# Two attention layers and an MLP on one core: where ScalarE and VectorE turn a norm's blocks, and where the second query weights are fetched

## The chip, the cores and the metric

One NeuronCore of a Trainium2 chip runs the whole program. The time is the device time of one execution in microseconds (us), as a median of several runs. Its engines are TensorE (PE in the profile; PEld is its weight load), VectorE (DVE), ScalarE (ACT), GpSimd (POOL) and SyncE (SP), whose only work here is to issue DMAs.

## The reference, cut to what matters

A batch of 8 items with 256 tokens of width 512 goes through a small linear attention (called the first attention here), two cross-attentions with 16 heads of 128, and an MLP of width 2048, each of the last three behind a layer norm.

```python
def _cross_attention(q_in, kv_in, wq, bq, wk, bk, wv, bv, wo, bo, bias_k, bias_v):
    qh = (q_in @ wq + bq).reshape(b, q_len, H, K)
    kh = (kv_in @ wk + bk).reshape(b, t, H, K)
    vh = (kv_in @ wv + bv).reshape(b, t, H, K)
    kh = jnp.concatenate([kh, broadcast(bias_k)], axis=1)
    vh = jnp.concatenate([vh, broadcast(bias_v)], axis=1)
    logits = jnp.einsum('bqhk,bthk->bhqt', qh, kh) / sqrt(K)
    weights = jax.nn.softmax(logits, axis=-1)
    ctx = jnp.einsum('bhqt,bthk->bqhk', weights, vh).reshape(b, q_len, H * K)
    return ctx @ wo + bo

def _forward(x, xf_1, xf_2, ...):
    x = x + _cross_attention(layer_norm(x), xf_1, ...)
    x = x + _cross_attention(layer_norm(x), xf_2, ...)
    return x + gelu(layer_norm(x) @ w_fc1 + b_fc1) @ w_fc2 + b_fc2
```

## The kernel before

Every fp32 product is made of three matmuls of fp32r parts (L582, L583, L584 of the profile): each operand is held as a high part and the rest, and something has to make the two parts. For data it is ScalarE that writes the high part and VectorE that writes the rest; for weights GpSimd writes both (a cast, L464, and a subtraction, L467).

The program has three stretches. The **front** (0 to about 796 us) makes keys and values of all heads, for both layers, and stores them in DRAM: a unit K is one block of keys, a unit V one block of values, and V units of the last group share TensorE's time with the start of the first norm. The **steps** (about 796 to 2031 us) are the attention: 64 steps s, 32 to a layer, each of two heads (a "body") for 512 tokens (a "chunk", of four). The **last part** is the MLP.

A step has four slots j = 0 to 3, and slot j of step s has item J = 4s + j, which is one head for 256 tokens. What TensorE does in a slot is written out by hand in `slot_order`, in this order: the logits of the item after (`L`, J + 1, tile S), the transposes of this item's probabilities (`T`, J, tile T), half of a projection, the product with the values of the item before (`P`, J - 1, tile O), and the other half. In slots 0 and 2 the projection is that of the next step's queries (`q`, from hT and the weights wqs); in slots 1 and 3 it is two tiles of the output projection (`w`, from oT and wos). All of these but L, T and P write one of four banks of PSUM, named U, used in turn: the unit numbered u waits until VectorE has taken what unit u - 4 left (`take`, semaphore `free`, which VectorE raises in the order of the units).

For an item J the chain is: logits (PE), `least_of` (DVE, L1032), `exponentials` (ACT, L848, two of them, with their sums), `inverted` (DVE, L1036), `divided`, which scales the item (ACT, L856, two), transposes (PE, L676), `turned_hi` (ACT, L866) and `turned_lo` (DVE, L1040), product (PE), `weighted_hi` (ACT, L875) and `weighted_lo` (DVE, L1047).

`norm_at(s)` names the steps that carry a norm too: s = 0 and 1 (the last two chunks of the first norm), 30 to 33 (all four chunks of the second) and 62 and 63 (the first two of the third). In such a step GpSimd's normalised rows z are transposed in four blocks, `Z` with ch = 0 to 3 (PE, L619, a U bank each): two in slot 1, one in slot 2 and one in slot 3. `rows(ch)` takes such a block: on ScalarE two operations (L815 scale and offset into aff, L818 the high part hT), on VectorE one (L1005, the rest of hT, both of whose inputs lie in SBUF). VectorE also gathers statistics for the next norm (`stats_of`, L944; `moments`, L950 and L952) in those steps whose following step has a norm, 29 to 32, 62 and 63.

GpSimd's queue (in program order, around step 0): `normalise(0, 2)`, then `queries(1)` (the parts of the second query weights, into wqs_b, which shares its place with the buffer tmp and so waits until all V units have been staged), then `normalise(0, 3)`, then `add_bias(0, 1)` to `(0, 3)`, twelve additions of a bias row to x (L536). `normalise(0, 3)` also waits for block 3 of the chunk before it to have been transposed, since z has one buffer. SyncE's queue is in order too; `load(0, use(E), wa[E])` fetches the query weights of body E into raw[0] and first waits for GpSimd to have split what lay there.

Of the kernel before, what the change touches and what calls it, by code (L numbers as in the profile page):

```python
# [50 lines left out]
GROUPS = HBODIES // 2  # L51
# [134 lines left out]
def bass_xattn(nc, x_in, ctx_in, thw, thb, pgw, pgb, www, bncol, wa, wk, wv, wb, hcol, vrow,  # L186
               lncol, f1col, orow, out):
    ctx = ExitStack()
    with ctx:
# [6 lines left out]
        def f(ap):  # L196

            return ap.bitcast(F32)
# [97 lines left out]
        def bank(*name):  # L296
            return U[:, UNIT[name] % RING, :]
# [32 lines left out]
        def use(E):  # L330

            return 2 * GROUPS + E
# [3 lines left out]
        def _(sp):  # L336
            def load(i, n, src):

                if n:
                    sp.wait_ge(split[i], n)  # L340
                sp.dma_start(raw[i][:], src).then_inc(raw_in[i], 16)

            def load_o(E):
                load(1, use(E), wb[E].rearrange("p c (a n) -> p (c a) n", n=256))

            def load_v(e):

                for i in range(2):
                    load(i, 2 * e + 1, wv[2 * e + i])
                if e:  # L350
                    sp.wait_ge(vb_ready, e)
                sp.dma_start(raw_vb[:].rearrange("p a b n -> p (a b) n"),
                             vrow[2 * e:2 * e + 2].rearrange("a b n -> (a b) n").partition_broadcast(P)).then_inc(vrow_in, 16)
# [36 lines left out]
            for what, *a in FRONT:  # L390
                if what == "K":
                    e, c, h = a
                    n = KV["K", e, c, h]
                    sp.wait_ge(free, UNIT["K", e, c, h] + 1)
                    sp.dma_start(kd[2 * e + h // 2, c, :, :, h % 2, :], f(stage[:, n % 4, :, :])).then_inc(sent[n % 4], 16)
                    if (c, h) == (2, 0):
                        if e + 1 < GROUPS:
                            for i in range(2):
                                load(i, 2 * e + 2, wk[2 * e + 2 + i])
                        else:  # L400
                            load(0, use(0), wa[0])
                            load_o(0)
                    if (c, h) == (3, 2) and 0 < e < GROUPS - 1:
                        load_x(e + 1)
                elif what == "V":
                    e, t = a
                    n = KV["V", e, t]
                    sp.wait_ge(staged, VS["V", e, t] + 1)
                    sp.dma_start(vd[e, t // 4, :, :, :, t % 4, :].rearrange("p g q n -> p (g q) n"),
                                 f(value_slots(n)).rearrange("p g q n -> p (g q) n")).then_inc(sent[n % 4], 16)  # L410
                    if t == 8 and e + 1 < GROUPS:
                        load_v(e + 1)
                    if t == 12 and e == 0:
                        load_x(1)
                    if t == 2 and e + 1 == GROUPS:

                        sp.wait_ge(z_x, TILES)
                        for i in range(4):
                            sp.wait_ge(sent[i], 16 * 8)
                        load_k(0)  # L420
                        load_values(0)
# [1 line left out]
                sp.wait_ge(sent[i], 16 * len(KV) // 4)  # L423
            load_k(1)
            load_values(1)
            load(0, use(1), wa[1])

            for E in range(HBODIES):
                for c in range(CHUNKS):
# [328 lines left out]
        def _(act):  # L758
# [47 lines left out]
            def rows(n, c, ch):  # L806
                k = (n * CHUNKS + c) * CH + ch
                act.wait_ge(unit, UNIT["Z", n, c, ch] + 1)
                if k > 1:
                    former = [u for u in UNIT if u[0] == "Z"][k - 2]  # L810
                    act.wait_ge(free, UNIT[former] + 1)
                else:
                    act.wait_ge(z_x, TILES)
                col = n * CH + ch
                act.activation(aff[:, k % 2, :], bank("Z", n, c, ch), ACT.Identity, bias=lnc[:, 1, col:col + 1],  # L815
                               scale=lnc[:, 0, col:col + 1]).then_inc(ln_affine, 1)
                act.wait_ge(ln_affine, k + 1)
                act.activation(hT[:, 0, ch, columns(c)], aff[:, k % 2, :], ACT.Copy).then_inc(ln_hi, 1)  # L818
# [76 lines left out]
            for s, j in SLOTS:  # L895
                J = 4 * s + j
                if j % 2 and s + 1 < STEPS:
                    queries(s + 1, j // 2)
                elif j % 2:
                    hidden(0, j // 2)  # L900
                turned_hi(J)
                if J + 1 < ITEMS:
                    exponentials(J + 1)
                z_of = norm_at(s)
                if z_of and j > 1:
                    rows(*z_of, j - 1)
                if J:
                    weighted_hi(J - 1)
                if J + 1 < ITEMS:
                    divided(J + 1)  # L910
                if z_of and j in (1, 3):
                    rows(*z_of, 0 if j == 1 else 3)

            for what, *a in last_order():
                if what == "P":
# [8 lines left out]
        def _(dve):  # L924
# [77 lines left out]
            def rows(n, c, ch):  # L1002
                k = (n * CHUNKS + c) * CH + ch
                dve.wait_ge(ln_hi, k + 1)
                dve.tensor_tensor(hT[:, 1, ch, columns(c)], aff[:, k % 2, :], f(hT[:, 0, ch, columns(c)]), ALU.subtract).then_inc(free, 1)  # L1005
# [63 lines left out]
            for s, j in SLOTS:  # L1069
                J = 4 * s + j  # L1070
                z_of, z_former, measured = norm_at(s), norm_at(s - 1), norm_at(s + 1) if s else None
                if j == 0 and s:
                    if z_former:
                        rows(*z_former, 3)
                    output("w", s - 1, 1)
                elif j == 2 and s:
                    output("w", s - 1, 3)
                if J + 1 < ITEMS:
                    least_of(J + 1)
                if j % 2 and s + 1 < STEPS:  # L1080
                    queries(s + 1, j // 2)
                elif j % 2:
                    hidden(0, j // 2)
                turned_lo(J)
                if j == 1 and s:
                    output("w", s - 1, 2)
                elif j == 3 and not z_of:
                    output("w", s, 0)
                if J + 1 < ITEMS:
                    inverted(J + 1)  # L1090
                if z_of and j > 1:
                    rows(*z_of, j - 1)
                if J:
                    weighted_lo(J - 1)
                if z_of and j == 1:
                    rows(*z_of, 0)
                if z_of and j == 3:
                    output("w", s, 0)
                if measured and s > 1:
                    for t in ((0, 1), (2,), (3,), ())[j]:  # L1100
                        stats_of(s - 1, t)
                    if j == 2:
                        moments(*measured)
# [77 lines left out]
```

## Time and profile before

| | us |
|---|---|
| median of 3 runs | 2394.86 |
| the three runs | 2382.49, 2394.86, 2408.23 |
| the profiled execution's own time | 2395.99 |
| its span, first to last instruction | 2394.1 |
| PE busy in the span | 2351.6 (98%) |
| DVE busy | 1339.3 (56%) |
| ACT busy | 1143.8 (48%) |
| POOL busy | 462.4 (19%) |
| mean granted clock of TensorE | 0.996 |

The profile is of one execution; 1.9 us of its time lie outside its span. Busy TensorE is not TensorE at its peak: an end is modelled, and at the lower of its two clocks (0.50 in the profile, 1.2 GHz) the same matmuls are busy for longer.

### The profile page before, as it was taken

What the parts mean: (1) busy time and instruction counts of PE and PEld (TensorE: products, weight loads), DVE (VectorE), ACT (ScalarE), POOL (GpSimd) and SP (SyncE); (2) the same over time, 40 slices, a digit from 0 to 9 for tenths busy, and PEclk for the clock granted to TensorE, in tenths of its full rate; (3) what the DMA queues carried; (4) which work ended last, traced back from release to release, by engine and by line L of the source; (5) the groups of instructions that cost most, each with busy time, mean ns of one, the idle gap of its engine ahead of it and who ended that gap; (6) DMA issues with size and microseconds to landing.
All of it is one profiled execution on the core that took longest, in us unless ns stands there. A gap on an engine that the chain in (4) does not pass through costs nothing.

```text
span 2394.1 us, 32423 instructions
## 1 busy us (share of the span) xinstructions
PE 2351.6 (98%) x12304; PEld 1997.9 (83%) x12304; DVE 1339.3 (56%) x2328; ACT 1143.8 (48%) x2717; POOL 462.4 (19%) x280
## 2 busy tenths in 40 slices
PE   8999999999999899999999989999999999999999
PEld 7888888888888788888888878888888887788887
DVE  4544445445445666666666676666666666644433
ACT  3222222222223566666666677666666667422222
POOL 2121112112123501111001244111001115611110
PEclk9999999999999999999999999999999999999999
DMA  7555656566556424333333333333333331100001
GB/s 272 197 196 203 230 195 215 202 217 227 191 203 212 168 98 143 127 115 136 125 137 124 124 107 119 133 116 134 126 139 124 123 134 45 44 18 27 27 1 70
DMA packets 142168, 331.83 MB, mean 139 GB/s; under 512 B 8896, under 2 KB 74944, under 8 KB 125632
## 3 DMA queue, kind: packets, MB, share of 16 engines
q1 hardware_dynamic: 141296, 329.68, 39.3%
q8 instruction: 99, 1.62, 0.3%
q14 instruction: 53, 0.43, 0.1%
q10 hardware_dynamic: 720, 0.10, 0.0%
HBM read 190.81 MB, written 138.94 MB: 138 GB/s over the span
## 4 chain that ended last, share of the span: by engine, by line
PE 90%; DVE 4%; ACT 4%; DMA 1%; issue 1%; POOL 1%; ACTq 0%; SPq 0%; DVEq 0%; POOLq 0%
PE U L582 23%; PE U L584 23%; PE U L583 23%; PE T L676 4%; PE O L582 2%; PE O L584 2%; PE O L583 2%; PE S L584 2%; PE S L583 2%; PE S L582 2%; DVE hT L1005 1%; ACT aff L815 1%; DVE gT L1015 1%; ACT probs L856 1%; ACT hT L818 1%
## 5 line engine op out<-in xcount | busy, mean ns | idle before, releaser
L1024 DVE TENSOR_TENSOR x<-x,U 128x512 f32<-128x512 f32 x384 | 260.9, 683 | 79.9 <-PE U L584 77.5
L848 ACT ACTIVATE probs<-S,nm 128x257 f32<-128x257 f32 x512 | 237.7, 476 | 37.4 <-DVE nm L1032 37.4
L1032 DVE TENSOR_REDUCE nm<-S 128x2 f32<-128x514 f32 x256 | 177.3, 692 | 123.6 <-PE S L584 119.8
L866 ACT ACTIVATE PT<-T 128x512 fp32r<-128x512 f32 x256 | 152.5, 596 | 173.9 <-PE T L676 173.4
L856 ACT ACTIVATE probs<-probs,rs 128x256 f32<-128x256 f32 x512 | 230.1, 500 | 1.4 <-DVE rs L1036 1.1
L797 ACT ACTIVATE stage<-U,hc 128x512 fp32r<-128x512 f32 x128 | 88.1, 689 | 286.9 <-PE U L584 286.9
L989 DVE SCALAR_TENSOR_TENSOR stage<-U,hc,stage 128x512 fp32r<-128x512 f32 x128 | 96.2, 751 | 223.4 <-ACT stage L797 223.4
L582 PE MATMUL U<-cT,wks 128*128 128x512 f32 x512 | 214.0, 418 | 2.0 <-DVE cT L967 2.0
L582 PE MATMUL U<-wos,oT 128*128 128x512 f32 x512 | 214.2, 418 | 0.4 <-DVE oT L1047 0.4
L804 ACT ACTIVATE stage<-tmp 128x512 fp32r<-128x512 f32 x128 | 81.0, 633 | 271.1 <-DVE tmp L997 271.1
L1047 DVE SCALAR_TENSOR_TENSOR oT<-O,hc,oT 128x256 fp32r<-128x256 f32 x256 | 123.8, 484 | 147.5 <-ACT oT L875 147.3
L464 POOL CAST wos<-raw 128x1024 fp32r<-128x1024 f32 x20 | 20.8, 1039 | 954.1 <-PE U L584 954.1
L584 PE MATMUL U<-wos,oT 128*128 128x512 f32 x512 | 203.0, 397 | 0.0
L583 PE MATMUL U<-wos,oT 128*128 128x512 f32 x512 | 202.1, 395 | 0.0
L582 PE MATMUL U<-wvs,cT 128*128 128x512 f32 x512 | 201.7, 394 | 0.0
L584 PE MATMUL U<-cT,wks 128*128 128x512 f32 x512 | 200.4, 391 | 0.0
L583 PE MATMUL U<-cT,wks 128*128 128x512 f32 x512 | 200.2, 391 | 0.0
L584 PE MATMUL U<-wvs,cT 128*128 128x512 f32 x512 | 199.4, 390 | 0.0
L583 PE MATMUL U<-wvs,cT 128*128 128x512 f32 x512 | 199.4, 389 | 0.0
L1040 DVE TENSOR_TENSOR PT<-T,PT 128x512 fp32r<-128x512 f32 x256 | 175.5, 685 | 42.3 <-ACT PT L866 42.3
L875 ACT ACTIVATE oT<-O,hc 128x256 fp32r<-128x256 f32 x256 | 121.2, 473 | 130.8 <-PE O L584 130.6
L676 PE MATMUL T<-ident,probs 128*128 128x128 f32 x1024 | 155.3, 274 | 13.5 <-ACT probs L856 13.4
(166 smaller groups left out, 5827.1 us busy)
## 6 DMA issues: line engine op xcount, KB each, us to landing
kd<-stage SPq DMA_DIRECT2D x128, 516.0 KB, 3.1
kb<-kd SPq DMA_DIRECT2D x64, 1032.0 KB, 4.8
vd<-stage SPq DMA_DIRECT2D x128, 512.0 KB, 3.2
vb<-vd SPq DMA_DIRECT2D x64, 1024.0 KB, 5.0
raw<-wa SPq DMA_DIRECT2D x24, 512.0 KB, 5.9
raw<-wb SPq DMA_DIRECT2D x24, 512.0 KB, 5.9
raw<-wk SPq DMA_DIRECT2D x16, 512.0 KB, 5.9
raw<-wv SPq DMA_DIRECT2D x16, 512.0 KB, 5.7
```

Source lines behind the costliest of these rows:

```text
L582: pe.matmul(o, lhs[0], rhs[0], start=start, stop=False)
L583: pe.matmul(o, lhs[0], rhs[1], start=False, stop=False)
L584: return pe.matmul(o, lhs[1], rhs[0], start=False, stop=stop)
L676: mm = pe.transpose(T[:, at_:at_ + P], probs[:, J % 2, qt, tt * P:tt * P + P], ident[:])
L848: ins = act.activation(probs[:, r, qt, 0:257], S[:, qt, 0:257], ACT.Exp, bias=nm[:, r, qt:qt + 1], scale=-1.0, accum_out=sums[:, r, qt:qt ...
L856: ins = act.activation(probs[:, r, qt, 0:256], probs[:, r, qt, 0:256], ACT.Copy, scale=rs[:, r, qt:qt + 1])
L866: act.activation(PT[:, J % 2, 0, :], T[:], ACT.Copy).then_inc(pt_hi, 1)
L875: act.activation(oT[:, 0, h, b * 256:b * 256 + 256], O[:, 0:256], ACT.Identity, bias=hc[:, 3, at_:at_ + 1]).then_inc(o_hi, 1)
L1024: dve.tensor_tensor(x[:, tile, :], x[:, tile, :], bank(what, s, t), ALU.add).then_inc(free, 1)
L1032: dve.tensor_reduce(nm[:, J % 2, :], S[:, :, 0:257], AX.X, ALU.min).then_inc(least, 1)
L1040: dve.tensor_tensor(PT[:, J % 2, 1, :], T[:], f(PT[:, J % 2, 0, :]), ALU.subtract).then_inc(pt, 1)
L1047: dve.scalar_tensor_tensor(out=oT[:, 1, h, to], in0=O[:, 0:256], scalar=hc[:, 3, at_:at_ + 1], in1=f(oT[:, 0, h, to]), op0=ALU.add, op1=AL ...
```

## The change

ScalarE: in a step with a norm, `rows` comes behind `weighted_hi` and `divided` in every slot: block 0 in slot 1 (as before), block 1 in slot 2, blocks 2 and 3 in slot 3. VectorE: `rows` comes behind `weighted_lo` in slots 2 and 3 too, with the same blocks as before. SyncE: the second query weights are fetched behind the store of V unit 5 of the last group, not behind all stores and the first four loads of keys and values.

```diff
@@ -410,6 +410,8 @@
                     if t == 8 and e + 1 < GROUPS:
                         load_v(e + 1)
+                    if t == 5 and e + 1 == GROUPS:
+                        load(0, use(1), wa[1])
                     if t == 12 and e == 0:
                         load_x(1)
@@ -423,7 +425,6 @@
             load_k(1)
             load_values(1)
-            load(0, use(1), wa[1])
@@ -902,14 +903,13 @@
                 z_of = norm_at(s)
-                if z_of and j > 1:
-                    rows(*z_of, j - 1)
                 if J:
                     weighted_hi(J - 1)
                 if J + 1 < ITEMS:
                     divided(J + 1)
-                if z_of and j in (1, 3):
-                    rows(*z_of, 0 if j == 1 else 3)
+                if z_of:
+                    for ch in ((), (0,), (1,), (2, 3))[j]:
+                        rows(*z_of, ch)
@@ -1088,12 +1088,10 @@
                 if J + 1 < ITEMS:
                     inverted(J + 1)
-                if z_of and j > 1:
-                    rows(*z_of, j - 1)
                 if J:
                     weighted_lo(J - 1)
-                if z_of and j == 1:
-                    rows(*z_of, 0)
+                if z_of and j:
+                    rows(*z_of, j - 1)
                 if z_of and j == 3:
```

ScalarE's queue in step 31, from slot 2's `rows` to slot 3's, before (from L827 on it is slot 3; L856 is `divided`):

```order
L815 ACTIVATE aff<-U,lnc 128x512
L818 ACTIVATE hT<-aff 128x512
L875 ACTIVATE oT<-O,hc 128x256
L856 ACTIVATE probs<-probs,rs 128x256 x2
L827 ACTIVATE qT<-U,hc 128x512
L866 ACTIVATE PT<-T 128x512
L848 ACTIVATE probs,sums<-S,nm 128x257 x2
L815 ACTIVATE aff<-U,lnc 128x512
L818 ACTIVATE hT<-aff 128x512
L875 ACTIVATE oT<-O,hc 128x256
L856 ACTIVATE probs<-probs,rs 128x256 x2
L815 ACTIVATE aff<-U,lnc 128x512
```

The same place in the changed kernel, whose lines there have one number more:

```order
L876 ACTIVATE oT<-O,hc 128x256
L857 ACTIVATE probs<-probs,rs 128x256 x2
L816 ACTIVATE aff<-U,lnc 128x512
L819 ACTIVATE hT<-aff 128x512
L828 ACTIVATE qT<-U,hc 128x512
L867 ACTIVATE PT<-T 128x512
L849 ACTIVATE probs,sums<-S,nm 128x257 x2
L876 ACTIVATE oT<-O,hc 128x256
L857 ACTIVATE probs<-probs,rs 128x256 x2
L816 ACTIVATE aff<-U,lnc 128x512
L819 ACTIVATE hT<-aff 128x512
L816 ACTIVATE aff<-U,lnc 128x512
```

The pair for block 1 has moved behind `divided` in slot 2, and the pair for block 2 behind it in slot 3, where it now stands ahead of the pair for block 3.

VectorE's queue in slot 2 of step 31, and the start of slot 3 (from L1032 on), before:

```order
L1036 RECIPROCAL rs<-sums 128x2
L1005 TENSOR_TENSOR hT<-aff,hT 128x512
L1047 SCALAR_TENSOR_TENSOR oT<-O,hc,oT 128x256
L944 BN_STATS stats<-x 128x6
L950 BN_AGGR mv<-stats 128x2 x4
L952 TENSOR_SCALAR vpe<-mv 128x4
L1032 TENSOR_REDUCE nm<-S 128x2
L1010 SCALAR_TENSOR_TENSOR qT<-U,hc,qT 128x512
```

and in the changed kernel:

```order
L1036 RECIPROCAL rs<-sums 128x2
L1047 SCALAR_TENSOR_TENSOR oT<-O,hc,oT 128x256
L1005 TENSOR_TENSOR hT<-aff,hT 128x512
L944 BN_STATS stats<-x 128x6
L950 BN_AGGR mv<-stats 128x2 x4
L952 TENSOR_SCALAR vpe<-mv 128x4
L1032 TENSOR_REDUCE nm<-S 128x2
L1010 SCALAR_TENSOR_TENSOR qT<-U,hc,qT 128x512
```

L1005 has changed places with L1047; the statistics and the next `least_of` still stand behind it.

SyncE's queue from the last V stores to the first steps, before (stores vd<-stage, keys kb, values vb, query weights raw<-wa):

```order
L409 DMA vd<-stage 512x1x256 x13
L370 DMA kb_55<-kd 128x2064
L375 DMA vb_56<-vd 128x2048
L341 DMA raw<-wa 128x1024
L370 DMA kb_62<-kd 128x2064
```

and in the changed kernel:

```order
L409 DMA vd<-stage 512x1x256 x3
L341 DMA raw<-wa 128x1024
L409 DMA vd<-stage 512x1x256 x10
L370 DMA kb_55<-kd 128x2064
L375 DMA vb_56<-vd 128x2048
L370 DMA kb_62<-kd 128x2064
```

The fetch of the weights now stands ahead of the last ten stores. GpSimd's and TensorE's queues are the same in both kernels.

## Rows read from the trace of the kernel before

**Rows 1.** TensorE's waits: us in total, times, the longest.

```profile
PE T L676 <- ACT probs L856: 13.4, 16, 2.9
PE U L619 <- DVE hT L1005: 6.0, 1, 6.0
PE U L619 <- POOL z L528: 2.7, 1, 2.7
```

**Rows 2.** Stretches of 100 us: busy us and instructions of each engine, clock, DMA.

```profile
800.00:900.00 100.00, 87.90 (x506) 75.78 (x505) 66.32 (x103) 63.80 (x165) 30.66 (x21) 0.93 0.35 124
...
1000.00:1100.00 100.00, 100.00 (x607) 88.77 (x606) 63.25 (x119) 66.92 (x184) 6.82 (x4) 1.00 0.38 133
```

**Rows 3.** GpSimd in order of time around step 0: start, us, instruction, idle before.

```profile
810.45 1.04 POOL L464 CAST wqs_b<-raw 128x1024 fp32r<-128x1024 f32 x1 [14.06 <-DMA raw<-wa]
...
815.60 8.65 POOL L528 TENSOR_SCALAR z<-x,mv,rstd 128x512 f32<-128x512 f32 x4 [0.18 <-POOL rstd L519]
824.22 14.83 POOL L536 TENSOR_TENSOR x<-x,brow 128x512 f32<-128x512 f32 x12
```

**Rows 4.** SyncE's fetch of the weights, VectorE's last V unit, stores, TensorE's block 3.

```profile
801.21 0.42 SPq L341 DMA_DIRECT2D raw<-wa  x1
...
796.09 0.69 DVE L1000 TENSOR_TENSOR stage<-tmp,stage 128x512 fp32r<-128x512 f32 x1 [0.98 <-ACT stage L804]
...
vd<-stage SPq DMA_DIRECT2D x128, 512.0 KB, 3.2
...
811.17 0.60 PE L619 MATMUL U<-ident,z 128*128 128x128 f32 x4
```

**Rows 5.** Step 1: VectorE's and TensorE's rows in order of time, and a stretch.

```profile
829.13 10.46 DVE L1005 TENSOR_TENSOR hT<-aff,hT 128x512 fp32r<-128x512 f32 x1 [1.64 <-ACT hT L818]
...
839.65 1.11 PE L619 MATMUL U<-ident,z 128*128 128x128 f32 x4 [5.99 <-DVE hT L1005]
...
844.00:846.00 2.00, 1.60 (x6) 1.51 (x7) 1.65 (x3) 1.37 (x3) 0.00 (x0) 0.50 0.00 0
```

**Rows 6.** ScalarE in slots 2 and 3 of step 31, and slot 0 of step 32.

```profile
1406.25 0.48 ACT L848 ACTIVATE probs<-S,nm 128x257 f32<-128x257 f32 x1 [1.58 <-DVE nm L1032]
...
1407.17 0.78 ACT L815 ACTIVATE aff<-U,lnc 128x512 f32<-128x512 f32 x1
1407.97 0.63 ACT L818 ACTIVATE hT<-aff 128x512 fp32r<-128x512 f32 x1
1408.51 0.46 ACT L875 ACTIVATE oT<-O,hc 128x256 fp32r<-128x256 f32 x1
1408.87 0.90 ACT L856 ACTIVATE probs<-probs,rs 128x256 f32<-128x256 f32 x2
...
1411.43 0.48 ACT L848 ACTIVATE probs<-S,nm 128x257 f32<-128x257 f32 x1 [0.33 <-DVE nm L1032]
...
1418.24 0.48 ACT L848 ACTIVATE probs<-S,nm 128x257 f32<-128x257 f32 x1 [1.47 <-DVE nm L1032]
```

**Rows 7.** VectorE in slot 2 of step 31, up to slot 3's `least_of`.

```profile
1408.64 0.69 DVE L1005 TENSOR_TENSOR hT<-aff,hT 128x512 fp32r<-128x512 f32 x1 [1.17 <-ACT hT L818]
1409.25 0.48 DVE L1047 SCALAR_TENSOR_TENSOR oT<-O,hc,oT 128x256 fp32r<-128x256 f32 x1
1409.64 0.68 DVE L944 BATCH_NORM_STATS2 stats<-x 128x6 f32<-128x512 f32 x1
...
1410.72 0.68 DVE L1032 TENSOR_REDUCE nm<-S 128x2 f32<-128x514 f32 x1
```

**Rows 8.** TensorE: the transposes of slot 3, step 31, and the logits of slot 0, step 32.

```profile
1409.82 0.66 PE L676 MATMUL T<-ident,probs 128*128 128x128 f32 x4 [1.18 <-ACT probs L856]
...
1419.31 0.39 PE L582 MATMUL S<-kb,qT 128*128 128x258 f32 x1 [0.16 <-ACT probs L848]
```

**Rows 9.** The second norm's additions on GpSimd, and VectorE's L1005 beside them.

```profile
1445.75 15.86 POOL L536 TENSOR_TENSOR x<-x,brow 128x512 f32<-128x512 f32 x12
...
1451.10 1.50 DVE L1005 TENSOR_TENSOR hT<-aff,hT 128x512 fp32r<-128x512 f32 x1 [1.64 <-ACT hT L818]
```

## The prediction, made before the changed kernel ran

> **What bounds the kernel now.** I read the busy shares first, then TensorE's waits, then stretches of time, then single queues where they dip. TensorE is busy for 2351.6 of 2394.1 us, so all that any edit here can win is its idle 42.5 us and the time it ran at its lower clock. Most of the waits in its list belong to steps with a norm [rows 1]: 13.4 us for `divided` in 16 pieces, one of 6.0 for VectorE's part of a block, one of 2.7 for z. A stretch of steps without a norm has no idle time at all, while the one around the first norm lacks 12.1 us [rows 2]. Only the eight steps with a norm, and the approach to the first, are in question.
>
> **The moved fetch.** GpSimd is idle for 14.06 us because the second query weights are not there [rows 3]; they are asked for at 801.21 us, behind everything else [rows 4]. `normalise(0, 3)` stands behind them and starts at 815.60 [rows 3], and TensorE waits 2.7 us for its z. Fetched with V unit 5, some 759 us into the span, they have landed long before. GpSimd's split then waits for the last staged V (796.09 + 0.69 = 796.8) [rows 4] and is done by about 800.3, since the cast and subtraction take 3.5 us. What is late next is the one buffer z: block 3 of step 0 is transposed at 811.17 [rows 4], and 0.7 us behind that z may be written, so at 811.9; if step 0's wait of 0.95 us for `divided` goes too, at 810.8. Instead of 815.60, `normalise(0, 3)` starts 4.8 us earlier, ends at about 819.4, and TensorE, which wants the block at 821.5, does not wait.
>
> That 4.8 is also what reaches the end, though TensorE is first ahead by only 4.5. The twelve additions follow z directly; beside them VectorE's L1005 of block 0 took 10.46 us instead of 0.69, up to 0.5 us behind the last of them (824.22 + 14.83 = 839.05), and TensorE waited 5.99 for its bank and then ran at 0.50 of its clock [rows 3, 5]. The additions now start at 819.4 and end at 834.2, so VectorE is free at 834.75, not 839.59. TensorE arrives about 4.5 us earlier and waits as long as before. The stall itself is not removed, it moves. Term: **-4.8 us**, between -2.7 (the z wait alone, nothing else moving) and -6.5 (that wait, the 1.7 us lost to the lower clock behind it, and one us more of the next).
> The fetch itself adds 512 KB ahead of ten stores; GpSimd split raw[0] at 743.5, so SyncE does not wait there. A store lands 3.2 us after its issue [rows 4] (up to 9.6 beside the first keys and values), its slot is used again four units later, over 11 us. Zero, with at most 1 us if it lands in that crowd.
>
> **The moved operations, one step.** Take step 31 [rows 6 to 8]; starts that have no row are the next ones of the same queues. Before, ScalarE goes from the exponentials (1406.25) through two exponentials and their sums (0.92), L815 and L818 (1.34), L875 (0.36) and L856 to a start of the transposes at 1409.82, for which TensorE had been ready at 1408.5. Without the pair L815 and L818, `divided` ends at 1408.43: the transposes start at 1408.5. That wins 1.3 us, as meant, in slot 2 of every step with a norm.
>
> It is given back in the same step. VectorE's next `least_of` stands behind L1005, and L1005 behind ScalarE's L818. Exponentials to exponentials, before: 0.92 + 0.80 (L815) + 0.67 (until VectorE starts) + 0.61 (L1005) + 0.39 (L1047) + 1.08 (statistics) + 0.71 (`least_of`) = 5.18, as in the rows (1406.25 to 1411.43). After: 0.92 + 0.36 (L875) + 0.80 (L856) + 0.80 + 0.67 + 0.61 + 1.08 + 0.71 = 5.95, L1047 now lying in VectorE's idle time. So the next exponentials come 0.8 us later, at 1412.2.
> Slot 3 to slot 0: before 6.81 (1411.43 to 1418.24): both pairs and L875 and L856 lie between, and VectorE's L1005 of block 3, a residual addition and `least_of` behind them. After, the same operations in another order: 6.8 to 6.9. TensorE's logits there waited for these exponentials before (1419.31, wanted at 1419.0), so they come 0.84 us later. Its banks say the same: the second tile of w in slot 3 needs VectorE's q (L1010, now 1412.1 + 0.7 = 1412.8, wanted at 1411.6), and slot 0's q needs block 2's bank, freed at 1416.5 and wanted at 1415.5, because L815 and L818 of block 2 now lie behind `divided`. From there the rest of the step hangs on ScalarE and VectorE as before. Term per step with statistics in slot 2: **+0.8 us**; the bounds are -1.3 (nothing is given back) and +1.6.
>
> Steps 30, 31, 32 and 62 are such steps: +3.3. Step 0 has no statistics: exponentials to exponentials was 4.76 there, held by the transposes, and is 4.86; slot 0's q waits 1.0 for block 2's bank: 0. Step 1, behind the stall, by the same reckoning ends 0.8 later, since TensorE had no wait left to lose. Step 33 had two waits, 1.37 for `divided` and 0.41 for oT, which both go, and gets most back in the bank wait: -0.5. Step 63 has no item behind it, so there `divided` is 1.3 earlier (the longest wait of rows 1, 2.9 us), and what follows is held by the gelu in between: -1.1. **Sum: -4.8 + 0 + 0.8 + 3.3 - 0.5 - 1.1 = -2.3 us** against 2395.99, the profiled execution, which is 1.1 above the median: on the median's scale 2392.5.
>
> **A rule against the rows.** GpSimd's additions and VectorE's L1005, both with two inputs in SBUF, get in each other's way. In step 1 L1005 was held through nine additions of 1.27 us [rows 5]; in step 33, beside the same twelve additions, it took 1.50, so it got in behind the one that was running [rows 9].
> The Trainium skill, SBUF — State Buffer, Who interferes with whom, says that a VectorE instruction with two SBUF inputs and a GpSimd instruction that reads SBUF exclude each other, the second to start being blocked until the first has finished, which is one instruction. By that rule the trace agrees in step 33 and not in step 1, and the stall of step 1 would not be there after the change.
>
> **Rivals.**
> *The stall is luck, and does not come back.* L1005 at 825.3 gets in behind a running addition. TensorE then meets block 2's bank without a wait. In a step without the stall the transposes are 2.81 us ahead of the next exponentials (1403.44 to 1406.25 in step 31), in step 1 it was 11.21 (829.62 to 840.83), so 8.4 less, and some 1.2 of the lower clock: -9.6 more, 2383. For it: step 33, and the three runs, which lie 12.4 and 13.4 us apart, about one such stall each. Against it: in the front a row of the same kind (L1000 at 773.27, 4.25 us, beside `add_bias(0, 0)`) was held too, two of two in the first norm.
> *One more stall: slower.* The additions of the second norm (1445.75, 15.86 us) lie beside steps 32 and 33; VectorE's L1005 of block 1 now comes a us later against them, and if it, or block 0's, is held through the rest, TensorE loses 5 to 10 us. It decides whether L1005 is let in behind a running addition. 2392.5 + 9.6 = 2402. For it: the run at 2408.23. Against it: two of two got in there before.
> *The reorder does what it is for.* If VectorE is less tight than I reckon, 1.3 us remain won in each of eight steps: -4.8 - 10.4 = -15.2, 2380. Against it is the sum 5.18, which is exact.
> *No effect at all.* The fetch moves GpSimd, but something else holds z; the reorder cancels: 2395.
>
> **How the numbers follow.** My forecast, within 5 us of 2392.5, has 0.50; no stall 0.20; one more stall 0.17; the full gain 0.06; no effect 0.07. All but the ends lie between 2379 and 2404, which leaves out about 0.15. Two runs of this kernel differ by up to 1%, 24 us, so 1% is about what can be told from no change, and nothing above reaches it: under 2371 needs the full gain and two stalls less, over 2419 needs two more stalls. Faster 0.04, same 0.92, slower 0.04.
>
> **What would show it.** Right: GpSimd's cast into wqs_b near 797, z of `normalise(0, 3)` near 811, no wait of TensorE for z. In steps 30 to 32, transposes of slot 3 without a wait, but waits for banks (U, behind DVE) or for exponentials in slot 3 and slot 0, and steps of 23.4 us instead of 22.6. Wrong: a cast that still waits; steps of 21.3 us; a total that moves by more than the stalls can.

## The result, and the profile after

The changed kernel is slower: 2403.55 us (median of 22 runs, 2394.34 to 2405.09) against 2396.2 (22 runs, 2382.49 to 2408.23), a ratio of 1.0038 with a 95% interval of 1.0028 to 1.0048. The forecast was 2392.5. The change is within the 1% that counted as no change, and the range (to 2404) just holds the time, but the kernel moved the other way than forecast. The runs come in groups: of before, five at 2382.5 to 2387.9, sixteen at 2394.7 to 2397.6, one at 2408.23; of after, 21 at 2401.6 to 2405.1 and one at 2394.34. The profiled execution of after took 2403.1 us with a span of 2401.2.

TensorE's waits in the changed kernel (us in total, times, the longest), which answer to [rows 1]:

```profile
PE U L620 <- DVE hT L1005: 11.4, 2, 6.2
...
PE S L583 <- ACT probs L849: 5.4, 7, 1.7
PE U L583 <- DVE hT L1005: 4.9, 6, 0.9
PE T L677 <- ACT probs L857: 4.0, 11, 1.5
PE U L583 <- DVE qT L1010: 3.9, 4, 1.0
```

The wait for z is gone and that for `divided` has shrunk from 13.4 to 4.0 us. The waits for exponentials have grown from 4.1 to 5.4 us, six for block 2's bank and four for q have come, and, above all, there are two long waits for L1005 instead of one.

**First norm.** GpSimd in order of time, which answers to [rows 3], then SyncE's fetch and VectorE's L1005 of block 0 in step 1, which answer to [rows 4, 5]:

```profile
796.17 1.04 POOL L465 CAST wqs_b<-raw 128x1024 fp32r<-128x1024 f32 x1
797.30 2.39 POOL L468 TENSOR_TENSOR wqs_b<-raw,wqs_b 128x1024 fp32r<-128x1024 f32 x1
...
809.81 8.27 POOL L529 TENSOR_SCALAR z<-x,mv,rstd 128x512 f32<-128x512 f32 x4 [9.13 <-PE U L620]
...
759.48 0.66 SPq L341 DMA_DIRECT2D raw<-wa  x1
...
824.59 8.91 DVE L1005 TENSOR_TENSOR hT<-aff,hT 128x512 fp32r<-128x512 f32 x1 [1.64 <-ACT hT L819]
833.42 0.68 DVE L1024 TENSOR_TENSOR x<-x,U 128x512 f32<-128x512 f32 x1
```

The cast no longer waits; z starts 5.79 us earlier (815.60 against 809.81), which is 4.8 counted from the start of step 0 in each trace, and waits for TensorE's block 3. L1005 is held until the twelve additions are over, as forecast.

**A step.** ScalarE's exponentials in step 31, slots 2 and 3, and step 32, slot 0, which answer to [rows 6], with what lies between the first two:

```profile
1401.80 0.48 ACT L849 ACTIVATE probs<-S,nm 128x257 f32<-128x257 f32 x1 [1.57 <-DVE nm L1032]
...
1402.71 0.47 ACT L876 ACTIVATE oT<-O,hc 128x256 fp32r<-128x256 f32 x1
1403.07 0.91 ACT L857 ACTIVATE probs<-probs,rs 128x256 f32<-128x256 f32 x2
1403.87 0.78 ACT L816 ACTIVATE aff<-U,lnc 128x512 f32<-128x512 f32 x1
1404.68 0.63 ACT L819 ACTIVATE hT<-aff 128x512 fp32r<-128x512 f32 x1
...
1407.75 0.48 ACT L849 ACTIVATE probs<-S,nm 128x257 f32<-128x257 f32 x1 [1.38 <-DVE nm L1032]
...
1415.08 0.48 ACT L849 ACTIVATE probs<-S,nm 128x257 f32<-128x257 f32 x1 [1.94 <-DVE nm L1032]
```

Exponentials to exponentials are now 5.95 us, to the hundredth what was forecast, and 7.33 to slot 0, not 6.8 to 6.9. Against before, the three lie 4.45, 3.68 and 3.16 us ahead: the step loses 0.77 in slot 2 and 0.52 in slot 3. Of the second loss, 0.47 us is in VectorE's row of block 3, the second L1005 here:

```profile
1411.35 0.69 DVE L1005 TENSOR_TENSOR hT<-aff,hT 128x512 fp32r<-128x512 f32 x1 [1.69 <-ACT hT L819]
1411.96 0.68 DVE L1024 TENSOR_TENSOR x<-x,U 128x512 f32<-128x512 f32 x1
1412.68 1.16 DVE L1005 TENSOR_TENSOR hT<-aff,hT 128x512 fp32r<-128x512 f32 x1
1413.77 0.67 DVE L1024 TENSOR_TENSOR x<-x,U 128x512 f32<-128x512 f32 x1
1414.37 0.68 DVE L1032 TENSOR_REDUCE nm<-S 128x2 f32<-128x514 f32 x1
```

VectorE reaches slot 3's two L1005 late and close together, and the second, which began 0.14 us into one of GpSimd's z operations (2.08 us each, the second at 1412.54), took 1.16 us. Before, both lay beside z too, but began over 1.3 us into an operation, and took 0.69.

**Second norm.** GpSimd's additions and VectorE's L1005 of block 0 in step 33, which answer to [rows 9], TensorE's block behind it, and the stretch behind that (busy us and instructions of PE, PEld, DVE, ACT and POOL, then clock, DMA share, GB/s):

```profile
1442.73 14.88 POOL L537 TENSOR_TENSOR x<-x,brow 128x512 f32<-128x512 f32 x12
1457.57 1.03 POOL L465 CAST wqs_b<-raw 128x1024 fp32r<-128x1024 f32 x1
...
1449.25 9.89 DVE L1005 TENSOR_TENSOR hT<-aff,hT 128x512 fp32r<-128x512 f32 x1 [1.65 <-ACT hT L819]
1459.07 0.68 DVE L1024 TENSOR_TENSOR x<-x,U 128x512 f32<-128x512 f32 x1
...
1459.20 1.12 PE L620 MATMUL U<-ident,z 128*128 128x128 f32 x4 [6.19 <-DVE hT L1005]
...
1456.00:1464.00 8.00, 3.57 (x15) 3.20 (x16) 5.67 (x7) 3.59 (x10) 5.28 (x4) 0.50 0.00 0
```

This is where the sign turns. L1005 took 9.89 us and not 1.50: held through seven additions and the cast behind them. TensorE waited 6.19 us and then ran at half its clock, 1.2 GHz.

How far the changed kernel is ahead (-) or behind (+), from the starts of the same `least_of` in both traces: -0.97 at the start of step 0, -5.75 from the end of step 2 to step 30, -1.85 in slot 1 of step 33, +6.15 in step 34, still +6.16 ahead of step 62, +7.1 at the end.

### The profile page after: what moved, and what is told of

Its sections match the earlier page's. It is cut to its first block, busy times and chain, and to the rows that moved or that the text cites. A ratio compares the mean times of both kernels' runs of the same rounds, so it can differ in the third digit from the quotient of the medians.

```text
span 2401.2 us, 32423 instructions
## 1 busy us (share of the span) xinstructions
PE 2352.7 (98%) x12304; PEld 1996.0 (83%) x12304; DVE 1345.8 (56%) x2328; ACT 1144.3 (48%) x2717; POOL 459.2 (19%) x280
## 4 chain that ended last, share of the span: by engine, by line
PE 89%; DVE 4%; ACT 4%; issue 1%; POOL 0%; DMA 0%; ACTq 0%; DVEq 0%; POOLq 0%
PE U L583 23%; PE U L585 23%; PE U L584 23%; PE T L677 4%; PE S L583 2%; PE S L585 2%; PE S L584 2%; PE O L583 2%; PE O L585 2%; PE O L584 2%; DVE hT L1005 2%; ACT aff L816 1%; ACT probs L857 1%; ACT probs L849 1%; DVE gT L1015 1%
## 5 line engine op out<-in xcount | busy, mean ns | idle before, releaser
L1032 DVE TENSOR_REDUCE nm<-S 128x2 f32<-128x514 f32 x256 | 177.4, 693 | 123.4 <-PE S L585 119.6
L1047 DVE SCALAR_TENSOR_TENSOR oT<-O,hc,oT 128x256 fp32r<-128x256 f32 x256 | 123.9, 484 | 147.0 <-ACT oT L876 146.3
L583 PE MATMUL U<-hT,wqs 128*128 128x512 f32 x384 | 155.8, 406 | 6.7 <-DVE hT L1005 4.9
```

The lines of the kernel that those rows point to most:

```text
L583: pe.matmul(o, lhs[0], rhs[0], start=start, stop=False)
L1032: dve.tensor_reduce(nm[:, J % 2, :], S[:, :, 0:257], AX.X, ALU.min).then_inc(least, 1)
L1047: dve.scalar_tensor_tensor(out=oT[:, 1, h, to], in0=O[:, 0:256], scalar=hc[:, 3, at_:at_ + 1], in1=f(oT[:, 0, h, to]), op0=ALU.add, op1=AL ...
```

## The experiments

All ratios are to the kernel before, run on the same chip; they weigh all runs, and where the runs fall in groups they differ from the quotient of two medians. The kernels were not all run on one chip: the medians of before beside them lie between 2395.57 and 2396.46 us, so a difference of two medians below is uncertain by about 1 us from that alone. The part of the program ahead of step 0 also ends up to 4 us apart from one profile to another (794.3 to 798.1 us), so rows are compared step by step, from the first `least_of` of one step to that of the next. "Late additions" names an edit that several share, and that takes the additions of chunks 2 and 3 away from beside the held L1005:

```diff
                 for c in range(1, CHUNKS):
+                    if c == 2 and n < LAYERS:
+                        pool.wait_ge(free, UNIT["Z", n, CHUNKS - 1, CH - 1] + 1)
                     add_bias(n, c)
```

(and the same for n = 0, where the first norm's additions stand.) GpSimd does them once VectorE has taken the norm's last block.

### The two halves of the change

`fetch_only` is before with SyncE's lines of the change alone.

> Only the fetch of the second query weights is moved; ScalarE's and VectorE's order is that of before. Theory A (the changed kernel is slow because VectorE's L1005 of step 33 is now held through the second norm's additions, and the reorder brought it there): everything ahead of step 30 as in the changed kernel within 1 us, no long L1005 in step 33, 2396.2 - 5 = 2391. Rival B (the earlier start of the additions, which the fetch causes, is what lets L1005 be held wherever it meets them): a long L1005 in step 33 here too, about 2400. Rival C (neither: the reorder's waits alone are the loss): 2391 too, so the next run is needed to part A from C.

Measured: 2391.52 us (11 runs: eight at 2390.1 to 2393.6, three at 2402.8 to 2403.2), ratio 0.9996 (0.9973 to 1.0018). L1005 in step 1 and in step 33:

```profile
823.82 10.16 DVE L1006 TENSOR_TENSOR hT<-aff,hT 128x512 fp32r<-128x512 f32 x1 [1.64 <-ACT hT L819]
...
1445.90 1.44 DVE L1006 TENSOR_TENSOR hT<-aff,hT 128x512 fp32r<-128x512 f32 x1 [1.64 <-ACT hT L819]
```

The fetch alone is worth 4.5 us by the medians, but the interval reaches 5 us to either side, since the runs fall in two groups 11 to 12 us apart. The profiled one has the first L1005 held and the second let in, as before had; from the start of step 0 to that of step 3 it gains 3.7 us.

`reorder_only` is before with ScalarE's and VectorE's lines of the change alone.

> Only the order of ScalarE and VectorE is changed, the fetch stays where it was. Theory A: steps 30, 31, 32 and 62 are 1.3 us longer each (5.2 in all), and L1005 of step 33 is held for about 10 us, which costs 8: 2396.2 + 5 + 8 = 2409. If it is not held there, 2401. Rival B: 2401. Rival C: 2408 without any long L1005 behind step 1.

Measured: 2396.76 us (11 runs: nine at 2394.3 to 2397.6, 2407.98 and 2409.59), ratio 1.0019 (0.9997 to 1.0041). That is neither number as a median. The profiled execution is the one at 2409.59, and has both held:

```profile
828.98 11.27 DVE L1004 TENSOR_TENSOR hT<-aff,hT 128x512 fp32r<-128x512 f32 x1 [1.64 <-ACT hT L818]
...
1455.92 9.87 DVE L1004 TENSOR_TENSOR hT<-aff,hT 128x512 fp32r<-128x512 f32 x1 [1.64 <-ACT hT L818]
```

So both held costs 2409.6 here, and nine of eleven runs lie 12 to 15 us below that, about one held L1005 fewer. No profile of one was taken, so which of the two was let in there isn't shown. By their times both are held in two of eleven runs with the reorder alone, in three of eleven with the fetch alone, and in 21 of 22 with both halves. Which half brings the hold to step 33 is left open.

### Without the held L1005

`fetch_late` is `fetch_only` with late additions, `after_late` the changed kernel with them.

> Fetch moved, old order of ScalarE and VectorE, and in the first and second norm GpSimd's additions for chunks 2 and 3 wait until VectorE has taken the norm's last block, so that no L1005 of these norms can meet more than four additions. Theory A: no L1005 over 3 us in steps 0, 1 and 30 to 33; the stall of step 1 and its time at the lower clock go, about 9.6 us: 2391 - 10 = 2381, and all runs within 2 us of each other, since the runs of before at 2386 would be those without a stall. If the long L1005 only shows a wait that something else ends, it stays at 2391.

> The changed kernel with the same late additions. Theory A: both held L1005 go, leaving the reorder's own price of 1.3 us in each of steps 30, 31, 32 and 62, less 1 in step 63: 4 to 5 us above the run with the fetch moved and late additions, so 2385 to 2386, that is 17 below the changed kernel. Rival C (the reorder's waits are the whole loss): it stays near 2400, 10 or more above that run.

Measured: `fetch_late` 2378.63 us (7 runs, 2377.49 to 2381.23), ratio 0.9939 (0.992 to 0.9958); `after_late` 2382.97 (11 runs, 2381.0 to 2384.91), ratio 0.9964 (0.9947 to 0.9982). Every L1005 of `after_late` (duration in ns: least, median, most):

```profile
L1009 DVE TENSOR_TENSOR hT<-aff,hT x48: 691/693/2851, 754.8 to 2049.1; 128x512 fp32r<-128x512 f32 x48
```

None is held through a row of additions, and the runs no longer fall in groups: 4 us from the least to the most, where before has 26. With the holding gone, the reorder costs 2382.97 - 2378.63 = 4.3 us. From step 31's to step 32's first `least_of` it is 22.60 us without it and 23.90 with it. That +1.3 stands in steps 30, 31 and 62; step 32 shows only +0.3, since the late additions have made it 0.9 us longer in the old order (25.72 against 24.78 in before); steps 0, 1 and 33 add 0.7 together, and from step 63 on 1.7 us come back.

`after_late1` is the changed kernel with late additions in the second norm alone.

> The changed kernel with the additions late in the second norm alone. Theory A: only the held L1005 of step 33 goes, that of step 1 stays: 2403.5 less 8 to 10, so 2394 to 2395, and a few runs at 2384 in which step 1's is not held. If the two stalls hang together, 2384 or 2403.

Measured: 2393.47 us (10 runs, 2393.12 to 2394.07), ratio 0.9995 (0.9984 to 1.0007). None of the ten was near 2384, as a few were expected to be.

```profile
825.68 8.89 DVE L1007 TENSOR_TENSOR hT<-aff,hT 128x512 fp32r<-128x512 f32 x1 [1.64 <-ACT hT L821]
...
1449.93 0.69 DVE L1007 TENSOR_TENSOR hT<-aff,hT 128x512 fp32r<-128x512 f32 x1 [1.64 <-ACT hT L821]
```

The held L1005 of step 33 costs 2403.55 - 2393.47 = 10.1 us, that of step 1 2393.47 - 2382.97 = 10.5. The first of these is more than the whole loss of the changed kernel. The rows say the same: step 33 takes 21.91 us here and 32.32 in the changed kernel, and every other step with a norm is within 0.4 us of it.

### What holds L1005

`after_one2` is the changed kernel with additions of one input, which leave the bias rows out of x:

```diff
-                    pool.tensor_tensor(x[:, t, :], x[:, t, :], brow[:], ALU.add).then_inc(ln_bias, 1)
+                    pool.tensor_scalar(x[:, t, :], x[:, t, :], 0.0, 0.0, ALU.add, ALU.add).then_inc(ln_bias, 1)
```

> The changed kernel with GpSimd's additions of the bias row replaced by a tensor_scalar with one input (x plus 0 plus 0), so the bias rows are left out of x; they follow each other directly and take about 2.07 us each, as the normalising rows of that form do, 25 us for twelve and not 15. Beside rows of that form L1005 took 0.69 to 1.16. If it takes two inputs on GpSimd's side to hold it, none is over 2.8 us, and the time is 2386 to 2389. If it is held by any row of GpSimd's that reads SBUF, it is held for up to 20 us in both norms: 2415 or more.

Measured: 2379.02 us (8 runs, 2377.42 to 2380.01), ratio 0.993 (0.9906 to 0.9954). Additions and L1005 of block 0, second norm:

```profile
1434.27 23.06 POOL L537 TENSOR_SCALAR x<-x 128x512 f32<-128x512 f32 x12
...
1440.83 0.69 DVE L1005 TENSOR_TENSOR hT<-aff,hT 128x512 fp32r<-128x512 f32 x1 [1.64 <-ACT hT L819]
```

GpSimd works for 23 us without a gap and this L1005 isn't slowed at all. Block 2's, which began 0.09 us into one of these operations, took 1.06 us in the first norm and 1.08 in the second, so they do get in its way, but none holds it. Every L1005 seen held through a row was beside operations with two inputs. (These are also of another kind, tensor_tensor and not tensor_scalar, which no run parts from the number of inputs.) The time lies below the expected 2386 to 2389, and 4 us below `after_late`. Those 4 us lie behind the start of step 63, where 381.1 us are left and not 385.2, while all steps ahead of it take the same within 0.3 us: there the third norm's additions are of the other form too, and its last four L1005 start 1.7 to 2.7 us sooner. Why that is worth 4 us in the last part was not looked into.

`after_gap2` puts a short GpSimd operation behind each addition of the changed kernel (`idle` is a new tensor that nobody reads):

```diff
                     pool.tensor_tensor(x[:, t, :], x[:, t, :], brow[:], ALU.add).then_inc(ln_bias, 1)
+                    pool.memset(idle[:, n * TILES + t, :], 0.0)
```

> The changed kernel, and behind each of GpSimd's additions of a bias row a memset of two elements a partition in a place that nothing reads, so that no addition follows directly on another. If L1005 is held because one addition's reads follow the other's without a gap, it gets in behind the running one: no L1005 over 3 us, and 2403.5 - 9.6 - 8.4 = 2385.5, plus at most 2 for the longer additions. If GpSimd goes first whenever it has work waiting, whatever the work is, L1005 is held as before or longer: 2403 to 2406.

Measured: 2390.32 us (10 runs, spread from 2385.88 to 2399.35), ratio 0.9975 (0.9953 to 0.9996).

```profile
823.19 1.71 DVE L1007 TENSOR_TENSOR hT<-aff,hT 128x512 fp32r<-128x512 f32 x1 [1.65 <-ACT hT L821]
...
1438.84 10.34 DVE L1007 TENSOR_TENSOR hT<-aff,hT 128x512 fp32r<-128x512 f32 x1 [1.64 <-ACT hT L821]
```

One let in, one held through seven additions with a memset between each two, and the cast behind them. A short operation in between makes holding rarer, by the times, but doesn't end it.

`later_l1005c` delays VectorE in step 33 of `fetch_only` by two rows of statistics into an unused tensor, to move L1005 against the additions.

```diff
                 if z_of and j == 1:
+                    if s == 33:
+                        for i in range(2):
+                            dve.bn_stats(idle[:, i, :], x[:, i, :])
                     rows(*z_of, 0)
```

> Fetch moved, old order, no late additions, and in step 33 alone VectorE does two statistics rows (1.2 us, their result unused) ahead of L1005 of block 0, so that it meets the second norm's additions 6.5 us behind their start, as in the changed kernel, and not 5.35. If where it meets them decides, it is held to the last of them, nearly 10 us: 2391.5 + 8 to 10 = 2400 to 2402 in nearly all runs, though nothing of the reorder is in it. If the reorder decides in another way, it is let in: 2391.5 to 2393.

Measured: 2392.65 us (10 runs: 2390.33 to 2404.35), ratio 0.9997 (0.9975 to 1.0019). The two rows (1446.19, 1.28 us) fell into time in which VectorE waited for ScalarE anyway:

```profile
1446.19 1.28 DVE L1100 BATCH_NORM_STATS2 idle<-x 128x6 f32<-128x512 f32 x2
...
1447.92 1.46 DVE L1007 TENSOR_TENSOR hT<-aff,hT 128x512 fp32r<-128x512 f32 x1 [0.45 <-ACT hT L820]
...
1442.55 7.98 POOL L538 TENSOR_TENSOR x<-x,brow 128x512 f32<-128x512 f32 x6
```

L1005 stayed 5.37 us behind the additions' start, so this run says nothing on its question.

`adds_2_later` and `adds_4_later` move the other side: short GpSimd rows ahead of the second norm's additions in the changed kernel, two or four (`range(2)` or `range(4)`; the four write bf16).

```diff
+                    if n == 1:
+                        for i in range(2):
+                            pool.tensor_scalar(idle[:, i, :], ident[:], 0.0, 0.0, ALU.add, ALU.add)
                     for c in range(1, CHUNKS):
                         add_bias(n, c)
```

> The changed kernel, with two short GpSimd rows (128 elements each, about 1.0 us together) in front of the twelve additions of the second norm. Those then start about 1.0 us later, and VectorE's L1005 of block 0, which came 6.5 us behind their start and was held, comes about 5.5 us behind it, where the kernel before had it let in (5.35). If the distance decides (theory A): L1005 of step 33 takes about 1.5 us and the kernel about 2393.5 us. If anything else in the changed order decides (theory B): it takes 9 us still and the kernel 2403.

> The same with four such rows: the additions start about 2.0 us later and L1005 comes about 4.5 us behind their start. Theory A: at 4.1 and 4.9 us behind, in the first norm, it was held, so it is held here, about 8 us, and the kernel takes about 2402 us. Theory B, held whatever the distance: the same 2402, so that only the pair with two rows tells them apart; let in with both would say that GpSimd's short rows, or chance, decide.

Measured: 2405.67 us (6 runs, 2404.19 to 2406.01), ratio 1.0052 (1.0033 to 1.0072), and 2406.03 (5 runs, 2404.58 to 2408.6), ratio 1.0057 (1.0036 to 1.0078). Of `adds_2_later`:

```profile
1445.04 14.88 POOL L538 TENSOR_TENSOR x<-x,brow 128x512 f32<-128x512 f32 x12
...
1450.33 11.12 DVE L1009 TENSOR_TENSOR hT<-aff,hT 128x512 fp32r<-128x512 f32 x1 [1.64 <-ACT hT L823]
```

L1005 now comes 5.29 us behind the additions' start, almost where before and `fetch_only` had it let in (5.35 and 5.36), and is held for 11.12; with four rows, at 4.09 us, for 12.29. So theory A in its coarse form, that L1005 is let in about 5.5 us behind the start, fails. The two rows missed the let-in places by 0.06 us, so a dependence as fine as that is not excluded. Held longer it costs more, 2.1 and 2.5 us over the changed kernel.

### The order of ScalarE and VectorE

`act_only_late` is `fetch_late` with ScalarE's new order, VectorE's order as before.

> Fetch moved, late additions, ScalarE in the new order and VectorE in the old one, where L1005 stands ahead of L1047. L1047 and least_of then both stand behind ScalarE's L818: from exponentials to exponentials 6.34 us instead of 5.95 with both in the new order and 5.18 with neither, and TensorE's w in slot 3 waits for L1047. So 0.4 us more than both in each of four steps: 2384.5, and more waits of TensorE for oT. If the order on VectorE did not matter it would be 2383.

Measured: 2397.87 us (10 runs, 2397.17 to 2400.72), ratio 1.0016 (1.0005 to 1.0027): a miss by 13 us. Its longest waits of TensorE:

```profile
PE U L587 <- DVE oT L1051: 9.7, 6, 1.8
```

From exponentials to exponentials it is 6.34 us in slot 2 of step 31, as expected. What the sum left out is that VectorE's `weighted_lo` (L1051 here), which stands behind L1005, now waits for ScalarE's part of the norm (L823 here) too, and that the output projection waits for oT in slot 3 as well. Against `after_late`, steps 0, 1, 30, 32 and 33 are 1.7 to 2.0 us longer each, 31 and 62 0.4, and from step 63 on it is 5.8 us. VectorE's part of the change is worth 14.9 us where ScalarE's is made.

`least_first` is `after_late` with the next `least_of` ahead of L1005, so that the exponentials don't wait for L1005: VectorE takes block 1 in slot 3, behind `least_of`, and in slot 0 `least_of` goes ahead of block 3.

```diff
@@ VectorE
+                if j == 0 and z_former:
+                    least_of(J + 1)
                 if j == 0 and s:
                     if z_former:
                         rows(*z_former, 3)
...
-                if J + 1 < ITEMS:
+                if J + 1 < ITEMS and not (j == 0 and z_former):
                     least_of(J + 1)
+                if z_of and j == 3:
+                    rows(*z_of, 1)
...
-                if z_of and j:
+                if z_of and j in (1, 3):
                     rows(*z_of, j - 1)
```

`least_oldact` is the same without ScalarE's new order.

> The changed kernel with late additions, and on VectorE the next item's least_of stands ahead of the norm's L1005: block 1 is taken in slot 3 behind least_of, and in slot 0 least_of comes ahead of block 3. If the reorder's price (2383.0 against 2378.6) is that least_of stands behind L1005 and so behind ScalarE's L818, it turns: from exponentials to exponentials 4.5 us in slot 2 instead of 5.18 before the change and 5.95 after it, and some 0.7 less in slot 3. TensorE then keeps at most the wait for block 2's bank, 1 us. Each of steps 30, 31, 32 and 62 is 1 to 1.4 us shorter than in the old order: 2373 to 2375. Rival (what costs is the banks of U taken later, whatever stands ahead of least_of): they are freed no earlier here, so 2382 to 2384.

> Fetch moved, late additions, VectorE with least_of ahead of the norm's L1005, and ScalarE in the old order. It tells whether ScalarE's reorder is worth anything once least_of is freed from L1005: TensorE's transposes of slot 3 wait for divided again (1.3 us in each of the steps with a norm). If they are independent: 2373.4 + 2 to 4 = 2376. If freeing least_of is all of the gain, 2373; if the old order on ScalarE makes least_of's lead useless, 2378.6, as with the fetch moved and late additions alone.

Measured: `least_first` 2373.41 us (4 runs, 2372.68 to 2375.22), ratio 0.9906 (0.9891 to 0.9921), the best version, ahead of both kernels; `least_oldact` 2376.62 (5 runs, 2375.37 to 2378.29), ratio 0.9921 (0.9892 to 0.9949). VectorE at slot 0 and slot 3 of `least_first`:

```profile
1398.36 0.69 DVE L1036 TENSOR_REDUCE nm<-S 128x2 f32<-128x514 f32 x1
1398.96 0.68 DVE L1009 TENSOR_TENSOR hT<-aff,hT 128x512 fp32r<-128x512 f32 x1
...
1402.40 0.68 DVE L1036 TENSOR_REDUCE nm<-S 128x2 f32<-128x514 f32 x1
1403.14 0.75 DVE L1014 SCALAR_TENSOR_TENSOR qT<-U,hc,qT 128x512 fp32r<-128x512 f32 x1
```

`least_of` no longer stands behind L1005, and step 31 is 21.71 us, 2.2 shorter than in `after_late`. With `least_of` freed, ScalarE's reorder no longer costs: the medians differ by 2376.62 - 2373.41 = 3.2 us in its favour, where both engines' reorder cost 4.3 with `least_of` behind L1005. That is not the 1.3 us a step it was made for: of the 4.0 us between the two profiles, 2.0 lie ahead of step 0, where the kernels are the same; step 32 gains 2.4, step 31 0.5, steps 30 and 62 lose 0.2 each. The gain is some 2 us and nearly all of it in one step.

## Why the prediction was wrong, by its own steps

**What bounds the kernel.** Right: the two traces differ only in and just ahead of steps with a norm.

**The moved fetch.** Right in mechanism and in size. The traces give -5.75 by the end of step 2 against a forecast of -4.0 (-4.8 and +0.8 for step 1). Of this, 0.97 was there ahead of step 0, which is chance as far as the runs show: 0.15 stood already at 773 us, and the rest goes with L1000, which in before had been held beside `add_bias(0, 0)` for 4.25 us and took 1.73 this time (with the fetch moved it was still held in seven of eleven profiles). The other 4.78 answer to the term of 4.8. That term held a part of the reorder: block 3 transposed sooner, 810.8 and not 811.9. Without it the prediction's own numbers give 815.60 - 811.9 = 3.7, and `fetch_only` shows 3.7. So the fetch is worth 3.7 and the two halves together 4.8, and the +0.8 put on step 1 did not come. "The stall itself is not removed, it moves" held in step 1. (The term's far bound, -6.5, is not the sum of the three parts it names, 2.7 + 1.7 + 1 = 5.4.)

**The moved operations.** Right in sign and mechanism, too small in size. The term of +0.8 a step came out as +1.3: slot 2 gave the 0.77 reckoned, and slot 3, put at 0 to 0.1, gave 0.52 more, since the second of two crowded L1005 took 1.16 us. I had taken durations from before and not asked which operation of GpSimd each moved one would now lie beside. Four such steps: +5.2, not +3.3. The gains put on steps 33 and 63, -0.5 and -1.1, did not come as forecast either: with late additions step 33 is 0.1 us longer with the reorder than without it, and from step 63 on the changed kernel gives back 0.3 (1.7 with late additions).

**The step that failed** is the second norm's L1005, left in the sum at its old 1.50 us: it took 9.89, and step 33 lost 8.0 us where the sum had -0.5. The rival "One more stall: slower" (0.17) is what happened, in the profile and, by their times, in 21 of 22 runs. Its price, put at 9.6, was measured as 10.1 (`after_late1`). The evidence I weighed against it, "two of two got in there before", was one profiled execution. The three times of before, 12.4 and 13.4 us apart, said already that the same code goes either way, and I read them so for the first norm while holding the second for settled. By the starts of `least_of`, the whole is -5.75 (first norm) + 3 x 1.3 (steps 30 to 32) + 8.0 (step 33, forecast -0.5) + 1.3 (step 62) - 0.35 (step 63 and behind, forecast -1.1) = +7.1, and the profiled executions differ by 2403.1 - 2395.99 = 7.1. Step 33 lost 8.0 and not 10.1, since before was no undisturbed norm either: its two L1005 of 1.50 and 1.79 us (the first in [rows 9], the second at 1456.22) lie together 1.9 us above twice 0.69, and its step 33 took 24.31 us where `fetch_late` has 21.77. (The sum for the ends of the range was off as well: at 9.6 each, 2419 would have needed three more stalls and not two, and 2371 the full gain with one stall less.)

**The rule against the rows.** The Trainium skill, SBUF — State Buffer, Who interferes with whom, has the second instruction blocked until the first has finished. Beside a single operation of GpSimd it holds: in the changed kernel's step 32 L1005 came 0.09 us into a weight's subtraction of 2.40 us and took 2.86, which ends 0.55 behind it:

```profile
1423.09 2.40 POOL L468 TENSOR_TENSOR wos<-raw,wos 128x1024 fp32r<-128x1024 f32 x1
...
1423.18 2.86 DVE L1005 TENSOR_TENSOR hT<-aff,hT 128x512 fp32r<-128x512 f32 x1 [1.64 <-ACT hT L819]
```

In step 33 it did not: seven additions and the cast passed. Beside one-input additions (`after_one2`) it wasn't blocked even for one, at most slowed to 1.08 us. The rival "the stall is luck" was right in that it is no fixed thing, and wrong as to which way this change turns it.

**What stays open** is what decides, at a given place, whether L1005 is held to the end of GpSimd's row or let in behind the running addition. Shown: it is held beside additions with two inputs (tensor_tensor) and not beside those with one (tensor_scalar); and the kernel's code alone does not fix which way it goes. For the last, take L1000 at about 773 us, in the front, where thirteen of the profiles have the same code on GpSimd and VectorE and L1000 begins 0.11 us into the second of four additions: it was held in nine and let in in four. One of each, before and in the changed kernel:

```profile
773.27 4.25 DVE L1000 TENSOR_TENSOR stage<-tmp,stage 128x512 fp32r<-128x512 f32 x1 [0.77 <-ACT stage L804]
...
773.12 1.73 DVE L1000 TENSOR_TENSOR stage<-tmp,stage 128x512 fp32r<-128x512 f32 x1 [0.77 <-ACT stage L805]
```

How far the running addition had got sorts most cases of L1005. For block 0 of the second norm it sorts all seven profiles that have twelve additions in a row without memsets: held at 0.28 to 0.34 us into one, let in at 0.35 and twice at 0.39. In the first norm it was held in six at 0.27 to 0.33, but also at 0.40 (`reorder_only`, step 1) and at 1.20 (before, step 1), and with memsets between it was let in at 0.13 and held at 0.12. So it is at best a part of the cause. Why the changed kernel falls on the held side in nearly all of its runs is not settled.

## What to carry to other kernels

A wait taken off one engine is worth nothing if another engine has the moved operation in front of what the chain needs next: `divided` came 1.3 us earlier and the exponentials 0.8 us later, until `least_of` was put ahead. Where two engines can hold each other, a profile of one execution shows one of its outcomes; look at how the times of several runs group before pricing it. And take such operations apart (here by letting additions that nobody waits for run later) before tuning the order around them: it won 13 us on `fetch_only` and 21 on the changed kernel, and the scatter went.

## What the runs showed of the hardware

VectorE's subtraction with both inputs in SBUF (0.69 us alone) was held for 8.9 to 12.3 us beside a row of GpSimd's two-input additions of 1.27 us each, until the row was over (step 1), and with it the cast that followed without a gap (step 33); with a memset of 0.11 us behind each addition it was still held in one of two norms. Let in in step 33, it took 1.4 to 1.8 us and the next addition 1.75 instead of 1.26. Beside one-input GpSimd operations of 1.92 us each it took 0.69 to 1.08. A held L1005 of 9 to 10 us cost some 10 us in total: 6.2 of TensorE waiting for the bank, the rest in the waits behind it and in matmuls at 0.50 of the clock.
